# An adaptive-layer-norm transformer block on one core: four edits to the order of work and one to where it is done

## What is computed

```
mod = (silu(c) @ wmod).reshape(4, 6, 1, 512)
sa, ca, ga, sb, cb, gb = mod[:, 0], mod[:, 1], ..., mod[:, 5]
ga = (2 * (ga >= 0) - 1) * max(abs(ga), 0.25)          # and gb likewise
h = layernorm(x) * (1 + ca) + sa
q, k, v = split(h @ Wqkv + bqkv)                       # 128 features each
x = x + ga * (softmax(q @ k.T / sqrt(128)) @ v @ Wo + bo)
h = layernorm(x) * (1 + cb) + sb
top1 = argmax(h @ gate_w.T + expert_bias)              # 4 experts
delta = lora_B[top1] @ (lora_A[top1] @ h)              # rank 8
x = x + gb * (h @ W_up.T + delta)
```

## Time and profile before

| what | value |
|---|---|
| time before, median of 3 runs | 190.87 us (190.68 to 191.09) |
| the profiled execution | 191.06 us, of which the span of its instructions is 189.1 us |
| PE | busy 176.1 us, 93% of the span |
| DVE | 138.0 us, 73% |
| ACT | 90.7 us, 48% |
| POOL | 79.4 us, 42% |
| DMA | 19.21 MB; its engines are busy nearly without a break from 5 to 33 us, little after that |
| granted TensorE clock, mean | 0.997 of full |

### The profile page before, as it was taken

The page is one execution under the profiler, slowest core; times in us unless marked ns, Lnnn a source line. Parts: engine busy times, 40 slices in busy tenths (PEclk is TensorE's granted clock), DMA queues, the critical chain, the costliest instruction groups (busy, mean ns, idle before and its releaser), DMA issues.

```text
span 189.1 us, 2847 instructions
## 1 busy us (share of the span) xinstructions
PE 176.1 (93%) x951; PEld 138.6 (73%) x951; DVE 138.0 (73%) x339; ACT 90.7 (48%) x172; POOL 79.4 (42%) x106
## 2 busy tenths in 40 slices
PE   6897999989998799998999999999999999989990
PEld 6873757867757578776888788788878887757870
DVE  1929758799989857797946678569476474987964
ACT  3356135954067979030856594213665602555110
POOL 3545200279143990008769910017694000342650
PEclk9999999999999999999999999999999999999998
DMA  4999997920033000050023300001140000001404
GB/s 170 364 389 387 388 309 171 359 43 14 0 80 143 3 2 0 2 168 3 0 111 122 100 3 0 0 0 57 58 142 25 3 0 3 0 0 55 160 36 192
DMA packets 12221, 19.21 MB, mean 102 GB/s; under 512 B 2812, under 2 KB 3328, under 8 KB 12208
## 3 DMA queue, kind: packets, MB, share of 16 engines
q1 hardware_dynamic: 12208, 19.05, 29.3%
HBM read 14.83 MB, written 4.21 MB: 101 GB/s over the span
## 4 chain that ended last, share of the span: by engine, by line
PE 59%; DVE 11%; issue 2%; ACT 1%; POOL 1%; DVEq 0%; POOLq 0%
PE bank L352 38%; PE bank L476 3%; PE bank L503 2%; PE bank L432 2%; PE bank L461 2%; PE bank L527 1%; PE bank L529 1%; DVE h2lo L1104 1%; PE bank L579 1%; DVE stats L969 1%; PE bank L455 1%; PE bank L458 1%; DVE xs L1158 1%; DVE stats L1165 1%; PE bank L366 1%
## 5 line engine op out<-in xcount | busy, mean ns | idle before, releaser
L1410 POOL TENSOR_TENSOR rstd<-var_eps,neg_half 128x1 f32<-128x1 f32 x16 | 8.8, 550 | 47.2 <-DVE var_eps L1169 47.2
L352 PE MATMUL bank<-wup_lo,h2hi 128*128 128x512 f32 x64 | 26.6, 416 | 0.0
L832 ACT ACTIVATE xn_p<-xs,shift,rstd 128x512 f32<-128x512 f32 x16 | 12.9, 814 | 27.5 <-POOL shift L1413 27.5
L352 PE MATMUL bank<-wup_hi,h2hi 128*128 128x512 f32 x64 | 25.2, 395 | 0.0
L352 PE MATMUL bank<-wup_hi,h2lo 128*128 128x512 f32 x64 | 25.2, 394 | 0.0
L352 PE MATMUL bank<-h1lo,wqkv_hi 128*128 128x512 f32 x48 | 19.8, 413 | 1.2 <-ACT wqkv_hi L825 1.2
L1425 POOL TENSOR_TENSOR xs<-xs,f_gb 128x512 f32<-128x512 f32 x14 | 17.9, 1290 | 7.2 <-DVE f_gb L1223 7.2
L1402 POOL TENSOR_TENSOR xs<-xs,gabo 128x512 f32<-128x512 f32 x16 | 20.3, 1295 | 0.1
L352 PE MATMUL bank<-h1hi,wqkv_hi 128*128 128x512 f32 x48 | 19.0, 396 | 0.0
L352 PE MATMUL bank<-h1hi,wqkv_lo 128*128 128x512 f32 x48 | 18.9, 394 | 0.0
L1387 POOL TENSOR_TENSOR wo_ga<-wo_raw,ga_bc 128x512 f32<-128x512 f32 x4 | 5.1, 1281 | 29.3 <-DMA ga_bc<-gates_dram 14.9
(11 more groups left out here) (178 smaller groups left out, 420.0 us busy)
## 6 DMA issues: line engine op xcount, KB each, us to landing
out_dram<-xs SPq DMA_DIRECT2D x16, 256.0 KB, 2.0
stage<-in_L_wmod_dram SPq DMA_DIRECT2D x3, 1024.0 KB, 7.6
xs<-in_L_wmod_dram SPq DMA_DIRECT2D x3, 1024.0 KB, 9.7
xs<-in_L_attn_x_dram SPq DMA_DIRECT2D x3, 1024.0 KB, 6.8
xs<-in_L_attn_x_dram SPq DMA_DIRECT2D x2, 512.0 KB, 3.8
f_gb<-in_L_ffn_W_up_dram SPq DMA_DIRECT2D x1, 1024.0 KB, 10.2
gb_bc<-gates_dram SPq DMA_DIRECT2D x4, 256.0 KB, 3.6
xn_p<-in_L_attn_Wqkv_dram SPq DMA_DIRECT2D x4, 192.0 KB, 8.6
```

The source lines that it names most:

```text
L352: mm = nc.tensor.matmul(dst, w, m, start=first and i == 0, stop=last and i == total - 1)
L832: nc.scalar.activation(xn2_p[:, t, :], xs[:, b, t, :], ACT.Identity, bias=shift[:, 1, t:t + 1], scale=rstd[:, 1, t:t + 1]).then_inc(S["xn2 ...
L1410: nc.gpsimd.tensor_tensor(rstd[:, 1, t:t + 1], var_eps[:, 1, t:t + 1], neg_half[:, 0:1], ALU.pow).then_inc(S["ln2_rstd"], 1)
```

## The change

Five edits, with what they need around them:

1. Start: PE makes ca's products after x's first tile, not after its third. DVE copies their rows out of PSUM, in place of ACT, and adds 1/4 to each of the four partial sums, so that the sum over them holds the 1 of 1 + ca and the separate addition goes. The transposes of x's last tile come behind those of ca.
2. Batch 0: three of the four `p_transposes` stand ahead of ga's matmuls (two before), and the plan of banks is another: x1T's last tile of batch 1 takes bank 7 in place of 5, the attention output O of batch 0 bank 5 in place of 7, and what follows is permuted.
3. lora_B's three copies go from DVE to POOL, into a space of their own (the later `gz`), and no longer wait for batch 1's transposes.
4. The last part of qkv of batch 1 comes ahead of batch 0's `x2_transposes`, `qkv_evacuate(1)` ahead of `h2_high(0)` and `qk_low(1)` ahead of `h2_low(0)`.
5. Batch 3's first statistics move from behind `choose_expert(0)` to ahead of `h1_low(2)`, and their normalising from behind `zT_evacuate(0)` to ahead of `o_high(1)`. In the last batch, the fourth `residual` and its statistics move ahead of `last_h2_low(0)`.

```diff
-        (2, "x1T", 1, 0), (4, "x1T", 1, 1), (6, "x1T", 1, 2), (5, "x1T", 1, 3), (7, "O", 0),
...
+        (2, "x1T", 1, 0), (4, "x1T", 1, 1), (6, "x1T", 1, 2), (7, "x1T", 1, 3), (5, "O", 0),
...
-        gz = sb("gz", [2 * GZ, T])
+        gz_home = sb("gz", [P, T])
+        gz = gz_home[0:2 * GZ, :]
...
-        lora_b_rep = xn1[:, 0, 0:NK * ZROWS].rearrange("p (k a z) -> p k a z", k=NK, a=3)
+        lora_b_rep = gz_home[:, 0:NK * ZROWS].rearrange("p (k a z) -> p k a z", k=NK, a=3)
...
-                return "mod_sum_ready", of[0] + 1
+                return "modT_ready", of[0] + 1
...
-                return "mod_sum_ready", (2, 3, 5, 7)[of[0]]
+                return "mod_sum_ready", (0, 1, 3, 5)[of[0]]
...
             keep_warm(bank[4], 8)
-            for t in range(NT - 1):
-                first_x1_transposes((t,))
-                keep_warm(bank[4], 2)
+            first_x1_transposes((0,))
+            keep_warm(bank[4], 2)
             modulation(0)
-            first_x1_transposes((NT - 1,))
+            first_x1_transposes((1,))
+            keep_warm(bank[5], 1)
+            first_x1_transposes((2,))
             first_modulation_columns(0)
             first_modulation_columns(1)
-            keep_warm(bank[5], 4)
+            first_x1_transposes((3,))
+            keep_warm(bank[5], 3)
             qkv(0, (0,))
...
             modulation_columns(2)
-            p_transposes(0, (0, 1))
+            p_transposes(0, (0, 1, 2))
             first_gate_everywhere()
             gate_to_rows("ga")
-            p_transposes(0, (2, 3))
+            p_transposes(0, (3,))
             x1_transposes(1)
...
             modulation_columns(3)
+            qkv(1, (3,))
             x2_transposes(0)
-            qkv(1, (3,))
             scores(1)
...
-            def first_modulation_rows():
-                act.wait_ge(S["mod_psum"], 1)
-                for half in range(2):
-                    part = slice(half * H // 2, (half + 1) * H // 2)
-                    nc.scalar.activation(mod_rows[:, 0, part], at("mod", 0)[:, part], ACT.Copy).then_inc(S["mod_rows_ready"], 1)
...
-            first_modulation_rows()
...
-            pt_high(0, (0, 1))
+            pt_high(0, (0, 1, 2))
...
-            pt_high(0, (2, 3))
+            pt_high(0, (3,))
...
+            qkv_evacuate(1)
...
-            qkv_evacuate(1)
...
                 pt_high(b)
+                if b == 1:
+                    ln1_normalise(3)
                 o_high(b)
...
                 zT_evacuate(b - 1)
-                if b + 2 < B:
-                    ln1_normalise(b + 2)
                 if not last:
...
-            def first_columns():
+            def first_modulation_rows():
+                dve.wait_ge(S["mod_psum"], 1)
...
-                    parts = at("caT", half)[:].rearrange("p (n q r) -> p n r q", n=NK, r=QUARTER)[:, :, 0:B, :]
-                    nts = slice(2 * half, 2 * half + 2)
-                    total = mod_sum[:, 0, half * 2 * B:(half + 1) * 2 * B].rearrange("p (n b) -> p n b", n=2)
-                    dve.wait_ge(S["modT_psum"], half + 1)
-                    nc.vector.tensor_reduce(total, parts[:, nts], AX_X, ALU.add).then_inc(S["mod_sum_ready"], 1)
-                    dve.wait_ge(S["mod_sum_ready"], half + 1)
-                    nc.vector.tensor_scalar(modT["ca"][:, nts, :], total, 1.0, None, ALU.add).then_inc(S["modT_ready"], 1)
-                dve.wait_ge(S["modT_ready"], 2)
+                    part = slice(half * H // 2, (half + 1) * H // 2)
+                    nc.vector.tensor_scalar(mod_rows[:, 0, part], at("mod", 0)[:, part], 1.0 / NK, None,
+                                            ALU.add).then_inc(S["mod_rows_ready"], 1)
+            def first_columns(half):
+                parts = at("caT", half)[:].rearrange("p (n q r) -> p n r q", n=NK, r=QUARTER)[:, :, 0:B, :]
+                nts = slice(2 * half, 2 * half + 2)
+                dve.wait_ge(S["modT_psum"], half + 1)
+                nc.vector.tensor_reduce(modT["ca"][:, nts, :], parts[:, nts], AX_X, ALU.add).then_inc(S["modT_ready"], 1)
...
-                dve.wait_ge(S["mod_sum_ready"], i + 2)
+                dve.wait_ge(S["mod_sum_ready"], i)
...
+                    if b == 0 and kt % 2 == 0:
+                        dve.wait_ge(S["modT_ready"], 1 + kt // 2)
...
+            first_modulation_rows()
...
-            first_columns()
-            h1_low(0)
+            first_columns(0)
+            h1_low(0, (0,))
+            first_columns(1)
+            h1_low(0, (1, 2, 3))
...
-            dve.wait_ge(S["x1T_psum"], 2 * NK)
-            dve.wait_ge(lora_b_in, 16 * E)
-            for a in range(3):
-                nc.vector.tensor_copy(lora_b_rep[:, :, a, :], lora_b_raw[:]).then_inc(S["loraB_rep_ready"], 1)
...
             ln1_moments(2)
+            qk_low(1)
             h2_low(0)
-            qk_low(1)
             for b in range(1, B):
...
                     gate_shift()
+                    ln1_stats(3, (0, 1, 2, 3))
+                    ln1_moments(3)
                 if not last:
...
-                if b + 2 < B:
-                    ln1_stats(b + 2, (0, 1, 2, 3))
-                    ln1_moments(b + 2)
...
                 else:
-                    for t in range(3):
+                    for t in range(NT):
                         residual(b, t)
...
                     last_h2_low(0)
-                    residual(b, 3)
-                    ln2_moments(b, 3)
                     last_h2_low(1)
...
+            pool.wait_ge(lora_b_in, 16 * E)
+            for a in range(3):
+                nc.gpsimd.tensor_copy(lora_b_rep[:, :, a, :], lora_b_raw[:]).then_inc(S["loraB_rep_ready"], 1)
...
+                if b == 1:
+                    ln1_deviation(3)
+                    ln1_offset(3)
...
-                if b + 2 < B:
-                    ln1_deviation(b + 2)
-                    ln1_offset(b + 2)
```

More of the change, by code:

```diff
@@ L51, in psum_plan @@
         (7, "PT", 0, 0), (1, "PT", 0, 1), (3, "PT", 0, 2), (0, "PT", 0, 3),
[1 row of a table removed]
-        (2, "wupT", 0), (4, "wupT", 1), (6, "wupT", 2), (5, "wupT", 3),
[1 row of a table added]
+        (2, "wupT", 0), (4, "wupT", 1), (6, "wupT", 2), (7, "wupT", 3),
         (1, "qkv", 1, 0), (3, "qkv", 1, 1), (0, "qkv", 1, 2),
-        (7, "Y", 0, 0), (4, "Y", 0, 1), (6, "Y", 0, 2), (5, "Y", 0, 3), (2, "mod", 3),
-        (7, "gateA"), (4, "loraB"), (2, "modT", 3),
-        (7, "x2T", 0, 0), (4, "x2T", 0, 1), (6, "x2T", 0, 2), (5, "x2T", 0, 3),
+        (5, "Y", 0, 0), (4, "Y", 0, 1), (6, "Y", 0, 2), (7, "Y", 0, 3), (2, "mod", 3),
+        (5, "gateA"), (4, "loraB"), (2, "modT", 3),
+        (6, "x2T", 0, 0), (7, "x2T", 0, 1), (5, "x2T", 0, 2), (4, "x2T", 0, 3),
         (7, "gzb"), (4, "gz", 0),
     ]
-    m, f = (0, 1, 3, 6, 5), (2, 7, 4)
+    m, f = (2, 1, 3, 0, 6), (5, 7, 4)
     for b in range(1, B):
@@ L79, in psum_plan @@
         else:
-            order += [(m[4], "x2T", b, 0), (m[1], "x2T", b, 1), (m[4], "x2T", b, 2), (m[2], "F", b, 0),
-                      (m[1], "x2T", b, 3), (m[0], "gz", b, 0), (m[3], "F", b, 1), (m[4], "zl", b, 0), (m[0], "gz", b, 1),
-                      (f[0], "zl", b, 1), (f[1], "F", b, 2), (m[1], "zT", b, 0), (f[2], "F", b, 3), (m[0], "zT", b, 1)]
+            order += [(m[4], "x2T", b, 0), (m[1], "x2T", b, 1), (m[3], "x2T", b, 2), (m[2], "F", b, 0),
+                      (m[0], "x2T", b, 3), (m[1], "gz", b, 0), (m[4], "F", b, 1), (m[3], "zl", b, 0), (m[1], "gz", b, 1),
+                      (f[0], "zl", b, 1), (f[1], "F", b, 2), (m[0], "zT", b, 0), (f[2], "F", b, 3), (m[1], "zT", b, 1)]
     place, earlier, holds = {}, {}, [None] * 8
@@ L817, in ln1_normalise @@
                         act.wait_ge(S["x1T_psum"], NK * b)
-                        if b == 2:
-                            act.wait_ge(S["loraB_psum"], 1)
                     nc.scalar.activation(xn1[:, t, :], xs[:, b, t, :], ACT.Identity, bias=shift[:, 0, t:t + 1],
```

## The result

| what | value |
|---|---|
| time after, median of 4 runs | 188.25 us (187.16 to 188.61), before 190.87 (190.68 to 191.09) |
| ratio to before, 95% interval | 0.9853, 0.981 to 0.9896 |
| the profiled execution | 188.43 us, of which the span is 186.3 us |
| the same kernel timed again, median of 6 runs | 187.81 us (187.09 to 188.82), ratio 0.9848 (0.9823 to 0.9874) |

What follows compares the result with a forecast made beforehand. PE bounds the kernel, busy 176 of 189.1 us. Terms 0.8 + 0.4 + 0.5 + 1.0 = 2.7, less 1.6 in a new wait, plus 0.9 and 0.9, win 2.9: median 188.0, likeliest 187.3 to 188.6, range to 189.4.

Steps and rivals of the forecast that it cites:

- Start, 0.8: At the start, ca's products begin at 9.9, the first `h1hi` at 13.0 instead of 13.79: 0.8 us won.
- that ca lands at 9.8: At the start, section ca's DMA, issued at 2.18, lands 7.6 later, at 9.8.
- The feared tie of the fourth tile with POOL: At the start, DVE's normalising of x's fourth tile may stand for POOL; losing twice costs all 0.8; rival's chance 0.15.
- Batch 0, 0.4 + 0.5 + 1.0: Batch 0: 0.4 from ga's columns, 0.5 from the gates' wait, 1.0 around `o_lo` with lora_B's copies off DVE.
- "nothing and 1.3 us each": Batch 0: bounds for each of lora_B's three copies on POOL; even 3.9 us in sum would end in time.
- qkv ahead: Batch 1's last qkv part ahead of x2T: waits of 0.5 for `xn2` and 0.9 for q and v go.
- "This lead can't be kept": Batch 1's scores end 4.7 ahead, but the other engines' own chain lets `gz_bias` come only 2.7 earlier, at 67.9.
- Batch 3's statistics: Ahead of batch 2's `h1lo`, they take 2.8 us; PE waits at batch 1's `p_transposes`, which end 1.1 ahead.
- The 0.9 from `o_lo`: Batch 1: the wait of 0.71 for `o_lo` and the restart go, 0.9; output projection 2.0 ahead.
- Last batch, 0.9: Last batch: wait of 1.4 for `xn2` goes, the first feed-forward product slips 0.7, fourth transposes start earlier: 0.9 won.
- The rival of the clock: TensorE's clock falls to 1.2 GHz around batch 1's new wait: 189.8, up to 191.6 at 7 us; chance 0.12.
- "3 to 4 us": How long the clock stays low in the mild case, each us costing 0.5, so 189.8.

Runs made afterwards that it cites:

- the profile without the fall: The changed kernel, unchanged, timed again; its profiled execution kept TensorE's clock at 1.00, span 184.9 us; median 187.81 us.
- the pair with the old start: The split version with PE's old start order and x's fourth tile normalised ahead of ca's rows, against the split version: 186.89 against 186.13 us.
- the split version: Changed kernel with batch 3's statistics divided: tiles 0 and 1 behind `plo`, tiles 2, 3 and moments behind `o_lo`; 186.13 us, ratio 0.9733.
- `qkv_back`: Changed kernel with batch 1's last qkv part, its copies and low part put back behind batch 0's second layer norm; 187.42 us, ratio 0.9829.
- the kernel alone: Kernel before the change with only batch 3's statistics, offset and normalising moved forward; 191.26 us, ratio 1.0018.
- the better place behind `plo`: Changed kernel with batch 3's statistics behind batch 1's `plo`, ahead of gb's rows, and the normalising behind `zT_evacuate`; 186.81 us, ratio 0.9789.
- the medians of the pair: The split version with the last batch's fourth residual and statistics again behind the first `h2lo`, against the split version: 187.03 against 186.13 us.
- `stats_back`: Changed kernel with batch 3's first statistics, their offset and normalising put back to their old places; 187.95 us, ratio 0.9841.

## Why the prediction was right, step by step

The time was right (188.0 predicted; 188.25 and 187.81 measured), by sound terms and by two errors of opposite sign. In the profile without the fall the change wins 4.2 us of the span (189.1 to 184.9), against 2.9 predicted: 0.7 more at the start, the rest in small parts behind it. The fall, which the sum left out, takes 1.3 of it again. So the mechanisms hold, but that the total does is in part luck.

- **Start, 0.8.** The mechanism held, and the median agrees: 0.76 in the pair with the old start. In the profile of the change it was 1.36, so the term was 0.5 too low: ca landed at 9.4, not 9.8, and `h1hi` started at 12.53, not 13.0. What failed is a sentence taken for granted, that ca lands at 9.8. Before, PE came at 11.25 and its landing was hidden; now it is what PE stands for, and in the nine profiles with the new start and the old order of DMAs ca's products began between 9.25 and 11.02. The feared tie of the fourth tile with POOL cost little: 0.79 us, for 0.57 in the split version, and no wait. The DVE copies of 256 columns start 0.4 apart or less (0.76 for two), as taken.
- **Batch 0, 0.4 + 0.5 + 1.0.** 2.7 ahead predicted behind the output projection; 3.4 measured (49.76 to 46.39), of which 1.36 is the start, so 2.0 for 1.9. PE waits 0.3 at `pv` for the gates, not 0.5. The third tile's transposes and the new banks were not undone by themselves; from the first product to `pv` it takes 22.65 (36.91 less 14.26), before 23.67 (39.29 less 15.62), so together they win 1.0 for 0.9. POOL's three copies take 0.77 together, near the lower bound of "nothing and 1.3 us each". POOL's `wo_ga` starts at 35.13, not at the 35.8 of the prediction, which left out the lead. Undoing this edit cost 1.2 to 1.6, somewhat more than the 1.0.
- **qkv ahead.** "This lead can't be kept" is what `qkv_back` shows. `gz_bias` was 3.3 ahead for 2.7 predicted, by the start's extra.
- **Batch 3's statistics.** `h1lo` at 70.02 (70.75 predicted), PE standing 2.1 (2 to 3), and the first product behind 1.44 ahead (1.1). Then the clock took 0.7 more over the next products: 0.73 ahead at gb's rows (78.05 before, 77.32). The 0.9 from `o_lo` came back: 1.63 at the output projection, for 2.0. In the kernel alone the move loses 0.4, without a fall; next to the better place behind `plo` it loses 1.0 to 1.4 by the medians, of which 0.5 is left between profiles without a fall.
- **Last batch, 0.9.** 0.9 by the medians of the pair, 1.3 by its profiles, 1.05 in the profile of the change.
- **The rival of the clock** had 0.12. In its mild form it came true in seven of ten runs, by their mean clock, and cost 1.3 us where a profile shows it, not 1.8 for "3 to 4 us". What failed is the weight, not the mechanism: the stand of 2.3 us and the half idle time behind it were written down, and given one chance in eight. One of the prediction's own signs of being wrong, products spaced 0.46 apart, came: the first three behind the transposes take 1.43 (73.75 to 75.18). The extra 0.5 of the start hid the error in the first median. The Trainium skill (TensorE: Matmul & The Clock Gate, "Why this matters for your kernels") advises against idle gaps between bursts of matmuls, and means longer ones than this stand of 2.08 us. Here the clock fell behind it in one profile and stayed up behind an equal one in the other, so the advice doesn't settle this case.
- **Open.** `stats_back` should be faster than the change by the fall and 0.5, as its profile has it, but its median is not; without the longest of its six runs it is 187.75, and these five still lie 2.5 us apart. The one of 189.11 has a mean granted clock of 0.989, so the clock may have fallen in it; the one of 188.15 has 1.0, and a late landing is only my guess for it.

## What to carry to other kernels

A lead that PE wins is worth what the other engines' chain lets it keep; before moving work forward on such an engine, look for the place behind the last result that PE wants and ahead of a gap (here behind `plo` and behind `o_lo`: 1.7 to 2.1 us better by the medians than ahead of `h1lo`, 1.3 of it without the clock's help). A wait of 2 us in a kernel at full clock should be priced with the clock, and a handful of useless matmuls was a cheap insurance here (0.6 to 1.1 us by the medians). When a consumer moves ahead of where it used to hide a transfer, take the transfer's spread for the new bound, not its one time.

## What the runs showed of the hardware

- TensorE's clock fell or not in the same program behind the same stand of 2.08 us; when it fell, it stayed at 1.2 GHz for about 3.4 us and cost 1.3 us. Where a fall of the same length came ahead of PE's wait for `h1lo`, the time from the first product grew by 0.15 us (`qkv_back`).
- The 1 MB of section ca, issued at 2.2, let PE's products begin between 9.25 and 11.02 us, while the DMA engines are busy without a break (a mean share of 0.98 to 1.06 in each us from 3 to 11 in the profile of the change).
- A copy of 128x128 from SBUF took 0.26 us on POOL (0.77 for three) at 31 us, with no wait, and 1.25 us on DVE while POOL ran additions. The Trainium skill (SBUF — State Buffer, "SBUF: two separate sides") says that a GpSimd instruction and a DVE one in a two-port mode shut each other out of a shared pair of ports; the DVE times fit this, and no run here takes POOL's additions away to prove it.
